# DLRM tower with a two-layer CIN: the half-filled K tile in two products, a new order of the first loads, and the copy of e on ScalarE two chunks later

## What is computed

```
e = stack([tbl_f[ids[:, f]] for f in range(39)], axis=1)        # (2048, 39, 16)
x = e
for W in (W0, W1):                                               # two CIN layers, 128 maps each
    inter = (x[:, :, None, :] * e[:, None, :, :]).reshape(B, last * 39, 16)
    x = einsum('bid,hi->bhd', inter, W)
    outs.append(x.sum(axis=-1))
h = concatenate([outs[0], outs[1], dense_ctx], axis=1)           # 128 + 128 + 16
h = relu(h @ W_top1 + b_top1); h = relu(h @ W_top2 + b_top2); y = h @ W_top3
```

## Time and profile before

| | |
|---|---|
| median of 3 runs | 783.21 us (782.36 to 785.63) |
| profiled execution, its own time | 780.78 us |
| its span | 779.0 us |
| busy: PE, DVE, POOL, ACT | 696.8, 674.9, 501.0, 420.2 us |
| moved by the 16 DMA engines | 115.67 MB, mean 148 GB/s |
| instructions | 17028 |

### The profile page before, as it was taken

How to read it: one execution, slowest core, us unless ns; L and a number is a source line. 1 busy time by engine, 2 the same in 40 slices (tenths; PEclk the granted TensorE clock), 3 DMA queues, 4 the chain that set the end, 5 groups by cost and what they waited for, 6 DMA issues and landing times.

```text
span 779.0 us, 17028 instructions
## 1 busy us (share of the span) xinstructions
PE 696.8 (89%) x6210; PEld 595.1 (76%) x6210; DVE 674.9 (87%) x864; ACT 420.2 (54%) x769; POOL 501.0 (64%) x406
## 2 busy tenths in 40 slices
PE   0222678999999999999999999999999999999997
PEld 0222455878888888888888888888888888888887
DVE  5653999999999999999999999999999999888810
ACT  0001465656566656557565656655566656575741
POOL 6777887878787877868787887888787850000000
PEclk9999899999999999999999999999999999999999
DMA  4369569696867777787869796777867695854000
GB/s 101 90 156 275 129 184 164 164 171 170 163 167 168 131 185 130 187 134 190 161 163 168 173 162 169 171 148 182 141 171 142 162 160 138 162 153 133 13 7 1
DMA packets 171030, 115.67 MB, mean 148 GB/s; under 512 B 135043, under 2 KB 146906, under 8 KB 170563
## 3 DMA queue, kind: packets, MB, share of 16 engines
q1 hardware_dynamic: 154750, 108.80, 60.3%
q0 software_dynamic: 12800, 3.30, 6.6%
q10 hardware_dynamic: 3397, 2.47, 1.1%
HBM read 104.08 MB, written 15.53 MB: 154 GB/s over the span
## 4 chain that ended last, share of the span: by engine, by line
PE 77%; POOL 7%; DMA 4%; DVE 4%; issue 4%; SPq 3%; ACT 0%; DVEq 0%; ACTq 0%; POOLq 0%
PE z_ps L424 18%; PE x_ps L384 12%; PE x_ps L388 11%; PE x_ps L385 11%; PE g_ps L414 8%; POOL e_rows L360 7%; PE x1T_ps L445 4%; PE aux_ps L373 4%; PE x1T_ps L403 3%; PE x1T_ps L437 2%; SPq L280 2%; PE x1T_ps L435 2%; DVE product_lo L676 2%; DVE products L668 2%; DMA e_scratch<-e_d 2%
## 5 line engine op out<-in xcount | busy, mean ns | idle before, releaser
L360 POOL DMA_INDIRECT e_rows<-in_tbl_dram,ids_sb x400 | 500.6, 1252 | 134.7 <-issue 119.8
L514 ACT CAST product_hi<-products 117x1024 fp32r<-117x1024 f32 (+1 forms) x256 | 242.6, 948 | 102.7 <-DVE products L668 101.7
L676 DVE TENSOR_TENSOR product_lo<-products,product_hi 117x1024 fp32r<-117x1024 f32 (+1 forms) x256 | 277.4, 1084 | 23.1 <-ACT product_hi L514 22.9
L668 DVE TENSOR_TENSOR products<-bases 117x1024 f32<-117x1024 f32 (+1 forms) x256 | 277.5, 1084 | 7.1 <-DMA bases<-eT_scratch 6.5
L384 PE MATMUL x_ps<-product_hi,w_hi 117*128 117x512 f32 x448 | 198.5, 443 | 14.2 <-ACT product_hi L514 10.4
L424 PEld LDWEIGHTS z_ps<-G,w1T 128*128 128x128 f32 x1248 | 165.0, 191 | 17.3 <-issue 0.5
L385 PE MATMUL x_ps<-product_hi,w_lo 117*128 117x512 f32 x448 | 178.2, 398 | 0.0
L424 PE MATMUL z_ps<-G,w1T 128*128 128x128 f32 x1248 | 178.1, 280 | 0.0
L388 PE MATMUL x_ps<-product_lo,w_hi 117*128 117x512 f32 x448 | 148.5, 401 | 19.0 <-DVE product_lo L676 19.0
L388 PEld LDWEIGHTS x_ps<-product_lo,w_hi 117*128 117x128 f32 x448 | 84.3, 190 | 43.6 <-DVE product_lo L676 23.7
L384 PEld LDWEIGHTS x_ps<-product_hi,w_hi 117*128 117x128 f32 x448 | 85.6, 191 | 28.4 <-issue 13.8
(11 more groups left out here) (55 smaller groups left out, 340.1 us busy)
## 6 DMA issues: line engine op xcount, KB each, us to landing
bases<-eT_scratch SPq DMA_DIRECT2D x155, 468.0 KB
e_diag<-e_scratch SPq DMA_DIRECT2D x512, 10.0 KB
id_spread<-id_scratch SPq DMA_DIRECT2D x16, 437.5 KB
e_rows<-in_tbl_dram,ids_sb POOLq DMA_INDIRECT x400
e_scratch<-e_d SPq DMA_DIRECT2D x16, 320.0 KB, 9.5
eT_scratch<-e_rows SPq DMA_DIRECT2D x16, 312.0 KB
eT_scratch<-eT_scratch SPq DMA_DIRECT2D x16, 312.0 KB
w1T<-in_L_rec_W_dram SPq DMA_DIRECT2D x1, 2496.0 KB, 19.3
```

The source lines that it names most:

```text
L360: nc.gpsimd.indirect_dma_start(out=e_rows[t % E_SLOTS][:, f * D:(f + 1) * D], out_offset=None, in_=tables[f], in_offset=bass.IndirectOffse ...
L514: nc.scalar.copy(product_hi[:, first:first + count, :], products[:, first:first + count, :]).then_inc(hi_ready, 1)
L668: nc.vector.tensor_tensor(products[:, first:first + count, :], bases[u % 2][:, b:b + count, cols], bases[u % 2][:, a:a + 1, cols].to_broad ...
L676: nc.vector.tensor_tensor(product_lo[:, first:first + count, :], products[:, first:first + count, :], product_hi[:, first:first + count, : ...
```

## The change

It has four parts.

1. **K tile 3.** The third block of K tile 3, whose rows hold the same products as its second block in another rotation, now gets lower weights in the table of weights (`w0_hi[:, 3]`), so that the first product also does the work of lower weights by higher part for block 1. A second set of weights (`w0_hi[:, 7]`) is for the lower part, whose third block is overwritten with the higher part of block 0 (`fill_mix`): it does lower weights by higher part for block 0. K tile 3 has 2 matmuls instead of 3; the second of them is the last one of the chunk and waits for the filling transfer. That transfer (39 rows of 2 KB, inside SBUF) is issued by ACT once for each chunk, after the rounding of group 2.
2. **Buffers.** The higher part of K tile 3 goes to two buffers by turns (tiles 3 and 7 of `product_hi`). The lower part stays single, so `lower_parts(g, 1)` now waits until all of chunk g-1 is contracted.
3. **First loads.** The bases of chunk 0 are issued by SP (sets 0, 2, 4) and ACT (sets 1, 3) together; SP waits until they have landed, and issues those of chunk 1 then.
4. **DVE's copies.** `copy_e` and the rounding of the dense inputs move from DVE to ACT. `copy_e(t+1)` is done at the end of chunk 4t+2 instead of in the middle of chunk 4t, and `store_e(t+1)` is issued in chunk 4t+3 instead of 4t. `copy_e(0)` stands ahead of ACT's first bases.

The prologue also gets five more weight transfers (39 instead of 34, on ACT's queue) and some small DVE operations that make the new weights.

```diff
@@ weights
-    for k, (a, b) in enumerate(PAIRS):
-        for n in range(2 if BASES[b] is MIXED else BLOCKS):
+    starts = [(BASES[a], BASES[b]) for a, b in PAIRS] + [(STARTS[0], (0, 13, 0))]
+    for k, (a, b) in enumerate(starts):
+        for n in range(BLOCKS):
@@ SP
-            load_base_part(sp, 0, 0, HB // 2, first_ready[0])
+            load_base_part(sp, 0, 0, HB // 2, first_ready[0], 0, 2)
+            sp.wait_ge(first_ready[0], 16 * LOADS)
+            load_base_part(sp, 0, HB // 2, HB // 2, first_ready[1])
...
                 if c == 0 and t + 1 < TILES:
                     store_eT(t + 1)
+                if c == 3 and t + 1 < TILES:
                     store_e(t + 1)
@@ PE, contract(g, n)
-                    nc.tensor.matmul(x1_ps[:, :], w0_hi[:, k, :], product_hi[:, k, :], start=(k == 0), stop=False)
-                    nc.tensor.matmul(x1_ps[:, :], w0_lo[:, k, :], product_hi[:, k, :], start=False, stop=False)
+                    nc.tensor.matmul(x1_ps[:, :], w0_hi[:, k, :], product_hi[:, mix_tile(g) if k == MIX else k, :],
+                                     start=(k == 0), stop=False)
+                    if k != MIX:
+                        nc.tensor.matmul(x1_ps[:, :], w0_lo[:, k, :], product_hi[:, k, :], start=False, stop=False)
                 pe.wait_ge(lo_ready, g * NG + n + 1)
                 for k in range(first, first + count):
-                    last = nc.tensor.matmul(x1_ps[:, :], w0_hi[:, k, :], product_lo[:, k, :], start=False, stop=(k == NT - 1))
+                    if k == MIX:
+                        continue
+                    last = nc.tensor.matmul(x1_ps[:, :], w0_hi[:, k, :], product_lo[:, k, :], start=False, stop=False)
+                if n == NG - 1:
+                    pe.wait_ge(mix_filled, 16 * (g + 1))
+                    last = nc.tensor.matmul(x1_ps[:, :], w0_hi[:, NT, :], product_lo[:, MIX, :], start=False, stop=True)
@@ ACT
+            def fill_mix(g):
+
+                act.wait_ge(hi_ready, g * NG + 2)
+                act.wait_ge(lo_ready, g * NG + 2)
+                act.dma_start(product_lo[2:R:BLOCKS, MIX, :].bitcast(f32),
+                              product_hi[0:R:BLOCKS, mix_tile(g), :].bitcast(f32)).then_inc(mix_filled, 16)
...
+            copy_e(0)
             act.wait_ge(eT_doubled, 16)
-            load_base_part(act, 0, HB // 2, HB // 2, first_ready[1])
+            load_base_part(act, 0, 0, HB // 2, first_ready[0], 1, 2)
...
+                if c == 1 and 0 <= t - 2 < TILES - 2:
+                    round_dense(t - 2)
                 if g < CHUNKS:
                     round_products(g, 2)
+                    fill_mix(g)
...
+                if c == 2 and t + 1 < TILES:
+                    copy_e(t + 1)
@@ DVE
+                if first <= MIX < first + count:
+                    after(dve, contracted, g * NG)
...
-                if c == 0 and t + 1 < TILES:
-                    copy_e(t + 1)
```

More of the change, by code:

```diff
@@ L58 @@
 NT = len(PAIRS)
+MIX = 3
+WT = NT + 1
 BLOCKS = 3
@@ L72, in after, with mix_tile, part_tiles @@
         engine.wait_ge(semaphore, value)
+def mix_tile(g):
+    return MIX if g % 2 == 0 else NT
+def part_tiles(g, n):
+    _, _, count, first = GROUPS[n]
+    if first + count - 1 == MIX:
+        return slice(first, mix_tile(g) + 1, mix_tile(g) - first)
+    return slice(first, first + count)
 def layer1_step(c, p):
@@ L146, in cin_tower @@
         products = sb("products", [R, NT, COLS])
-        product_hi = sb("product_hi", [R, NT, COLS], f32r)
+        product_hi = sb("product_hi", [R, WT, COLS], f32r)
         product_lo = sb("product_lo", [R, NT, COLS], f32r)
@@ L235, in cin_tower, with load_base_part @@
         y_stored = sem("y_stored")
-        def load_base_part(queue, t, first, count, ready):
+        def load_base_part(queue, t, first, count, ready, begin=0, step_of=1):
             at = first % HB * D
-            for a, starts in enumerate(BASES):
+            for a in range(begin, LOADS, step_of):
+                starts = BASES[a]
                 step = starts[1] - starts[0]
@@ L513, in round_products @@
                 after(act, contracted, (g - 1) * NG + n + 1)
-                nc.scalar.copy(product_hi[:, first:first + count, :], products[:, first:first + count, :]).then_inc(hi_ready, 1)
+                if first <= MIX < first + count:
+                    after(act, contracted, (g - 1) * NG)
+                nc.scalar.copy(product_hi[:, part_tiles(g, n), :], products[:, first:first + count, :]).then_inc(hi_ready, 1)
+            def fill_mix(g):
[3 more added lines that the diff above has]
+                              product_hi[0:R:BLOCKS, mix_tile(g), :].bitcast(f32)).then_inc(mix_filled, 16)
             def copy_x1(g):
@@ L556, in copy_y, with copy_e, round_dense @@
                 nc.scalar.copy(y, mlp_ps[0:1, 2, :]).then_inc(y_ready, 1)
+            def copy_e(t):
+                act.wait_ge(gathered[t % E_SLOTS], (t // E_SLOTS + 1) * 16 * len(GATHERED))
+                act.wait_ge(looked_up, (t + 1) * sum(map(len, SETS)))
+                after(act, e_stored, 16 * t)
+                nc.scalar.copy(e_d[:, :, 0:F], e_rows[t % E_SLOTS][:, :].rearrange("b (f d) -> b d f", d=D)).then_inc(e_d_ready, 1)
+            def round_dense(t):
+                act.wait_ge(dense_loaded, (t + 1) * 16 * 3 * GAP // D)
+                after(act, h1_in_ps, M1 * t)
+                nc.scalar.copy(dense_parts[:, :], dense_now[:, :]).then_inc(dense_hi_ready, 1)
             for n, f in list(enumerate(LOOKED))[NS // 2:]:
@@ L675, in lower_parts @@
                 after(dve, contracted, (g - 1) * NG + n + 1)
+                if first <= MIX < first + count:
+                    after(dve, contracted, g * NG)
                 nc.vector.tensor_tensor(product_lo[:, first:first + count, :], products[:, first:first + count, :],
-                                        product_hi[:, first:first + count, :].bitcast(f32), ALU.subtract).then_inc(lo_ready, 1)
-            nc.vector.memset(staging[0:R, 0:2 * NT * H + H1], 0.0).then_inc(zeroed, 1)
+                                        product_hi[:, part_tiles(g, n), :].bitcast(f32), ALU.subtract).then_inc(lo_ready, 1)
+            nc.vector.memset(staging[0:R, 0:2 * WT * H + H1], 0.0).then_inc(zeroed, 1)
             for n in range(2):
@@ L687, in _ @@
             nc.vector.tensor_copy(k_number[:, :], numbers_i[:, 1:1 + MAX_K])
+            third, rounded, block_no, is_last, is_other = (block_of[:, n:n + 1] for n in range(5))
+            nc.vector.tensor_scalar(third, numbers_i[:, 0:1], 1.0 / BLOCKS, -1.0 / BLOCKS, ALU.mult, ALU.add).then_inc(block_made, 1)
+            dve.wait_ge(block_made, 1)
+            nc.vector.tensor_single_scalar(third, third, 12582912.0, ALU.add).then_inc(block_made, 1)
+            dve.wait_ge(block_made, 2)
+            nc.vector.tensor_single_scalar(rounded, third, -12582912.0, ALU.add).then_inc(block_made, 1)
+            dve.wait_ge(block_made, 3)
+            nc.vector.scalar_tensor_tensor(block_no, rounded, -float(BLOCKS), row_number[:, :], ALU.mult, ALU.add).then_inc(block_made, 1)
+            dve.wait_ge(block_made, 4)
+            nc.vector.tensor_single_scalar(is_last, block_no, float(BLOCKS - 1), ALU.is_equal).then_inc(block_made, 1)
+            nc.vector.tensor_single_scalar(is_other, block_no, float(BLOCKS - 1), ALU.is_lt).then_inc(block_made, 1)
             for n in range(2):
```

49 lines of the change are left out of this document (29 added, 20 removed).

## The result

The changed kernel takes 808.85 us in the median of 4 runs (800.97 to 810.45), beside 783.17 us for the kernel before (782.36 to 785.63): a ratio of 1.0302, 95% interval 1.0231 to 1.0374. It is **slower**, by 25.7 us, outside the forecast range of 763 to 800. The profiled execution took 810.45 us, with a span of 808.6.

What follows compares the result with a forecast made beforehand. PE bounds the kernel, SP's queue some 2% behind. Chunk 8 at 149.2, twelve tiles at SP's 42.7 us to 661.6, then 117.42 less 1.9: span 777.1, profiled 778.9, median forecast 781 us, range 763 to 800.

Steps and rivals of the forecast that it cites:

- rival B: Last matmul of a chunk waits for a late filling transfer: 43.6 us a tile, time 794 us, slower; chance 0.15.
- the rule: Trainium skill: an engine takes turns between queue rows packet by packet, so ACT's fill passes SP's long loads; no size.
- SP's cycle: SP's queue, per tile: 41.65 + 0.85 for store_e + 0.2 for fills = 42.7 us (41.65 to 44.25), setting the pace.
- The start: Before chunk 4: DVE freed of its 11 us wait, tile 1 late; chunk 4 opens at 107.3 instead of 112.01.
- as before 5.3 us to the doubling: Tile 1 in SP's queue: from the gather's landing near 83 to the doubling, 5.3 us as before (79.80 to 85.13).
- a sign against it: Prologue: tile 1's gather landing at 80 or earlier, instead of about 83, would show the start forecast wrong.
- which bytes are ahead: First loads: the bytes queued ahead decide, not issue time; sharing chunk 0's loads gives nothing at the end.
- the gain turned into waiting for bases: Each tile: SP's 42.7 us exceeds PE's 41.5, so DVE waits for bases about 1 us at most tiles' first chunk.
- The upper bound of 0.76 us for the fills: SP's queue between bases and doubling: 0.32 MB of fills a tile at 163 GB/s cost 0 to 0.76 us, taken 0.2.
- PE's 41.5 us: PE alone per tile: 42.42 less 0.94 us, for one of 21 matmuls saved in each chunk.
- DVE's new wait at nothing: DVE's lower part of group 1 waits for PE to leave the chunk before; costed at nothing, cover thin at c = 1.
- ACT hidden: ACT's copy and casts, about 1 us a tile, and 0.84 us of fill issue per chunk cost no time.

Runs made afterwards that it cites:

- fastest kernel: Changed kernel with K tiles 2 and 3 formed first, fill issued earlier, two lower buffers, old first loads, one dense transfer instead of six: 771.98 us, ratio 0.9885.

## Why the prediction was wrong

**The sign fell with one sentence**, in rival B: that by the rule ACT's transfer passes SP's long loads, lands in time, "I give the rule the better half". The mechanism, its place at the last matmul of a chunk and what it would show were all written down; it got 0.15. The forecast's own sum has 0.2 us a tile for the filling transfers in SP's cycle and no term at all for a wait of PE on one of them. From 160 to 700 us the trace has 15.1 us of such waits and 34 us at half clock, and a tile takes 44.11 us where the sum had 42.7. The row of the gather (9.85 us beside SP's loads) was the nearest row to the fill, and it was right: the fill took 8.8 us in the chunk shown, where it met bases.

**B's price was too low, 794 us against 808.85.** Most of that lies before chunk 8: of the 18.9 us between its span and 808.6, 14.7 are there (chunk 8 at 147.0 against 161.7; without the fill it opens at 155.3), 6.1 in the tiles (43.6 us against 44.11), and the end was 1.9 shorter. It looked for the worst place at c = 1, where PE is fastest; the waits are at c = 2 and c = 0, where bases are issued. The time until the matmul is due matters less than what is in flight. And it counted the wait once, where the clock makes 3.2 us of 1.75.

**The parts.** Put into the kernel before one by one, the K-tile change costs 10.4 us, the new order of the first loads 6.4, the copies on ACT 4.1 (within their noise). That is 20.9 of the 25.7 us; the rest comes with the parts together.

**The start** was to give 4.7 us at chunk 4 and took 2.8. SP was to stand 2 to 4 us before w1T; it went out 12.4 us later than before, of which 7.8 are SP's wait for the first half. The step that failed is "as before 5.3 us to the doubling": it took 17.9, with w1T's 2.5 MB just ahead of the eT store. The gather landed at 78.5, which the prediction had named as a sign against it. Its remark that what decides is which bytes are ahead was right, and was not applied to this store.

**SP's cycle, 42.7 us, and the gain turned into waiting for bases**: not in this kernel, where SP waits for PE. With the fill taken away the bound is the one forecast: 42.46 us a tile, and from 160 us on waits for bases of up to 4.8 us. That the total fits too, 780.13 us against 781, is in part luck: chunk 8 opens at 155.3, 6.1 us later than in the sum, the tiles give back 2.9 and the end 2.9. In the copy of e alone, where SP waits for nothing but the eT store, the cycle is 42.86 us, near the 42.7. Its terms are not confirmed one by one: the issue of `store_e` at its new place took 0.45 us and not 0.85, and from the eT store's issue to the doubling it took about 1 us longer than before. The upper bound of 0.76 us for the fills does not follow from the numbers beside it: 0.32 MB at 163 GB/s are 2.0 us a tile, of which 19.7 of 42.4 us would get 0.9.

**PE's 41.5 us** is reached in the run without the fill. In the fastest kernel it is 41.93 against 42.54 in undisturbed tiles of the kernels without the K-tile change: 0.61 of the 0.94 predicted. A part of the rest is new with the earlier fill: its issue stands ahead of the relus in ACT's queue, and PE waits for them 2.1 us in 12 waits from 160 to 700 us, 0.17 us a tile, which no kernel with the fill at its old place shows. For what is left these runs don't tell the reason.

**DVE's new wait at nothing**: beside a late fill probably wrong. With two lower buffers the median is 14 us lower and a tile 0.9 us shorter, but in the twelve tiles PE also spent 17 us at half clock instead of 34, which is 8.5 of the 10.7 us gained; how much of that is the buffer's these runs don't tell. **ACT hidden**: right as far as tried; in the run with the copy of e alone DVE waits 2.9 us for `product_hi` from 160 to 700 us, before 15.0, and with one transfer of dense 8.2 us for ACT's rounding of dense, while PE sets the pace.

**Still open**: why the old order of the first loads, and w1T later, also make the tiles shorter (42.9 and 42.6 us instead of 44.1), when that order alone adds nothing to a tile of the kernel before. The waits for the fill from 160 to 700 us fell with them from 15.1 us to 10.0 and 8.4. In the twelve tiles all waits of PE fell from 17.6 us to 12.2 and 11.7, and the time at half clock from 34 us to 17 and 14. Half of that time is lost, so waits and clock together account for 14 of the 14 us gained by the one and 16 of the 18 by the other. Why the waits are fewer is what stays open. A shift of SP's loads against the fill would do it; it was not tried by itself.

## What to carry to other kernels

Before a small transfer is put on the path of the busiest engine, look up which large ones are issued in the 6 us before it, at every place of the period; give it a use that can wait as long as the slowest row of a like transfer, or issue it earlier. A freed issue slot is worth something only where its queue doesn't wait at that place anyway, and a gain on the first bound is worth what the second one leaves: here the fill had to be earlier, the first loads back in their old order and six small issues one before the saved matmul showed in full.

## What the runs showed of the hardware

**How long ACT's transfer stands behind SP's.** In the stretch 232 to 237 us of the kernel after, right behind the fill's issue, and in 237 to 240, the packets of SP's queue (q1) and ACT's (q10): number, MB, share of the 16 engines:

```profile
q1 hardware_dynamic: 256, 0.95, 69.0%
q0 software_dynamic: 56, 0.02, 14.7%
...
q1 hardware_dynamic: 240, 0.60, 75.3%
q10 hardware_dynamic: 52, 0.08, 10.2%
```
